# Two row gathers of a large expert slot, held back until the next small slot's first and last gelu

## The reference, cut to what matters

```python
xn = _layernorm(x)
g, v, d = xn @ Wg + bg, xn @ Wv + bv, xn @ Wd + bd
scan = linear_scan(sigmoid(g) * tanh(v), 0.001 + 0.998 * sigmoid(d))
scores = sigmoid(xn @ Wg_.T + bg_ + bias);  top 2 of 8 -> weights[T, E]
h  = gelu(einsum('td,ehd->teh', xn, W1) + b1)
eo = einsum('teh,edh->ted', h, W2) + b2
out = x + scan + gelu(xn @ Ws1.T + bs1) @ Ws2.T + bs2 + einsum('ted,te->td', eo, weights)
```

## Time and profile before

| what | value |
|---|---|
| time, 3 runs | median 681.78 us (680.64 to 683.04) |
| the profiled execution | 678.43 us, of it 676.6 us span |
| mean granted TensorE clock in it | 0.994 |
| busy share of the span | PE 95%, DVE 76%, ACT 64%, POOL 42% |

### The profile page before, as it was taken

The page is one execution under the profiler, slowest core; times in us unless marked ns, Lnnn a source line. Parts: engine busy times, 40 slices in busy tenths (PEclk is TensorE's granted clock), DMA queues, the critical chain, the costliest instruction groups (busy, mean ns, idle before and its releaser), DMA issues.

```text
span 676.6 us, 19821 instructions
## 1 busy us (share of the span) xinstructions
PE 642.1 (95%) x6246; PEld 505.7 (75%) x6247; DVE 513.3 (76%) x1328; ACT 435.6 (64%) x774; POOL 281.4 (42%) x263
## 2 busy tenths in 40 slices
PE   4899999999999999799999999999999999999993
PEld 3465757575656666588888888888888888888893
DVE  4899899999999989878666666666667667666772
ACT  6987786969696965455555545565566565656562
POOL 2133333324241515634454535344454636354432
PEclk9999999999999999999999999999999999999997
DMA  7525344342525141423333345355655666575622
GB/s 244 203 52 168 95 126 100 119 128 90 154 86 164 63 122 36 129 54 52 69 55 63 55 117 169 63 126 135 173 168 147 175 159 191 143 180 148 193 33 29
DMA packets 63264, 80.77 MB, mean 119 GB/s; under 512 B 19492, under 2 KB 55268, under 8 KB 60376
## 3 DMA queue, kind: packets, MB, share of 16 engines
q1 hardware_dynamic: 48072, 62.08, 28.8%
q0 software_dynamic: 15120, 17.77, 15.6%
HBM read 38.66 MB, written 18.10 MB: 84 GB/s over the span
## 4 chain that ended last, share of the span: by engine, by line
PE 79%; DVE 9%; issue 5%; ACT 3%; DMA 3%; DVEq 1%; POOL 0%; POOLq 0%; SPq 0%; ACTq 0%
PE bank L1320 30%; PE bank L1312 29%; PE bank L1300 7%; PE bank L1348 4%; PE bank L1371 3%; PE bank L1390 2%; DVE arena L941 2%; DVE arena L940 2%; DVE W L844 1%; ACT arena L641 1%; PE bank L1291 1%; DMA arena<-in_gates 1%; DVE arena L883 1%; PE bank L1256 1%; DMA out<-arena,slot_adds 1%
## 5 line engine op out<-in xcount | busy, mean ns | idle before, releaser
L1320 PE MATMUL bank<-W,arena 128*128 (+1 forms) x2112 | 277.1, 273 | 5.4 <-DVE arena L941 4.9
L1312 PE MATMUL bank<-rows,W 128*128 128x256 f16 (+1 forms) x1728 | 272.7, 296 | 4.7 <-issue 3.0
L641 ACT ACTIVATE arena<-bank,par 128x256 f32<-128x256 f32 (+2 forms) x344 | 164.5, 516 | 111.3 <-PE bank L1312 74.4
L1320 PEld LDWEIGHTS bank<-W,arena 128*128 128x128 f16 x2112 | 200.9, 98 | 42.1 <-issue 6.9
L1312 PEld LDWEIGHTS bank<-rows,W 128*128 (+1 forms) x1728 | 164.8, 98 | 58.9 <-issue 7.9
L555 POOL DMA_INDIRECT out<-arena,slot_adds x71 | 115.3, 1624 | 186.7 <-ACT arena L766 130.6
L940 DVE TENSOR_SCALAR arena<-arena,par 128x256 f16<-128x256 f32 (+1 forms) x284 | 102.3, 360 | 57.6 <-ACT arena L641 46.4
L941 DVE SCALAR_TENSOR_TENSOR arena<-arena,par 128x256 f16<-128x256 f32 (+1 forms) x284 | 133.9, 472 | 10.0
L499 POOL DMA_INDIRECT lists<-entry,place x64 | 70.6, 1103 | 125.1 <-ACT arena L623 66.5
L1300 PE MATMUL bank<-rows,W 128*128 128x512 f16 x288 | 63.8, 379 | 0.0
L647 ACT ACTIVATE rows<-bank 128x1024 f16<-128x1024 f16 (+2 forms) x43 | 36.1, 840 | 37.5 <-PE bank L1390 24.9
(11 more groups left out here) (189 smaller groups left out, 574.7 us busy)
## 6 DMA issues: line engine op xcount, KB each, us to landing
stage<-in_w SPq DMA_DIRECT2D x32, 512.0 KB
stage<-W SPq DMA_DIRECT2D x14, 1024.0 KB
arena<-W SPq DMA_DIRECT2D x8, 1024.0 KB
arena<-in_x SPq DMA_DIRECT2D x8, 512.0 KB
xhl_rows<-W SPq DMA_DIRECT2D x8, 512.0 KB, 3.7
out<-arena SPq DMA_DIRECT2D x8, 512.0 KB
b2row<-in_b SPq DMA_DIRECT2D x22, 128.0 KB
arena<-in_b SPq DMA_DIRECT2D x21, 128.0 KB
```

The source lines that it names most:

```text
L641: ins = A(h32[k][:, c], ps_e[k][:, c], ACT.Gelu, bias=p[:, 4 + e * i + jj:5 + e * i + jj], scale=p[:, 0:1])
L1312: ins = T.matmul(bank_, weights(w, wp * HALF + c * H + j * P, P), rhs[:, 2 * xp + c, :], start=n == 0, stop=n == 3 * KD - 1)
L1320: ins = T.matmul(banks[t // 2][:, (t % 2) * D:(t % 2 + 1) * D], h[:, hp, t * P:(t + 1) * P], weights(w, (2 + wp) * HALF + j * D, D), start ...
```

## The change

Inside `gather`, ahead of each of the two indirect DMAs of a large slot, a wait on `ev_act` is added, for large slots from 19 on. `small` is the slot after the one whose buffer is taken over (slot 16 for the gather of slot 19). The first DMA waits for the first gelu unit of `small`, the second for its last. Nothing else is changed: no DMA is added or taken away, and the order on GpSimd stays.

```diff
@@ -539,6 +539,10 @@
                     pool.wait_ge(r_ok, 2 * SEQS)
                 pool.wait_ge(rows_list_in[s.c], s.n // DEEP * 16 + 16)
                 for t in range(s.tiles):
+                    if s.rows == ROWS and s.n - DEEP >= FIRST + 1:
+
+                        small = order(s.n - DEEP + 1)
+                        pool.wait_ge(ev_act, RING + EV_A + small.unit + (1 if t == 0 else small.units))
                     pool.indirect_dma_start(
                         xg[s.c][0:s.parts, t, :], None, xhl_dram,
```

## The result

The changed kernel takes 674.54 us (673.96 to 674.79, five runs) against 683.04 us (680.64 to 683.86, five runs) for the kernel before: a ratio of 0.9879, with a 95% interval of 0.9859 to 0.9899. The prediction had 681.4 (679.8 to 683.4). The profiled execution of the changed kernel took 674.79 us, like its median; that of before, 678.43, was 4.6 us better than its own. So the two profiles show 3.6 of the 8.5 us, and the rest lies in executions that have no trace.

The account below looks back on a forecast made before the run. PE, busy for 95% of the span, was taken as the bound. Waits cost 0 and two freed splits save 0.21 + 0.21 us: 681.78 - 0.42 = 681.4 us, range 679.8 to 683.4.

Parts of the forecast that it names:

- The waits cost nothing: Gathers and scatter-adds delayed on GpSimd in LOW and MID turns would not make PE wait: cost 0.
- The held L940: In MID turns a GpSimd DMA lengthens DVE's split L940; freeing it would save 0.21 + 0.21 = 0.42 us in two turns.
- The reading of 475.97: PE's 0.40 us wait before 475.97 in the MID turn was put on the held L940 delaying L941; 0.21 us to gain.
- Nothing that the profile shows: Weight loads in the small slots' first layers wait 0.8 us with "issue" as cause, which nothing in the profile explains.
- the ceiling on the gain: All PE waits at L1371, the small slots' second layer, gone: 2.0 us, which gives the range's lower end, 679.8.
- Rival D: Faster: L1371's 2.0 us and the 0.8 us of "issue" waits go, as they fall beside gathers' traffic; 679.0, chance 0.10.
- That offset: The profiled execution of the kernel before took 678.43 us, 3.35 under the median of 681.78.
- A: Slower: moved DMAs hold slot 19's second split beyond PE's cover, up to 0.33 us in six MID turns; 683.8, chance 0.08.
- B: Slower: every L940 inside a moved gather is held to its end, twelve, 2.9 us less 0.4; 684.3, chance 0.02.
- C: No effect: PE's waits in MID turns come back at another place; 681.8, chance 0.20.

Follow-up runs that it names:

- e14: The kernel before with the second gather of each large slot from 19 on cut from 128 rows to 32: 680.98 us beside 681.37, ratio 0.9995.
- e0: The kernel before, unchanged, run again for a second profile: 673.86 us beside 674.04, ratio 0.9998.

## Why the prediction was wrong

**The waits cost nothing: right.** The second gather of slot 19 and scatter-add 15 came within 0.2 us of the forecast. The first gather of slot 19 went 1.0 us later (454.25 for 453.27). The second gather of the MID turn and scatter-add 17 behind it came 1.9 us earlier on the clock, because ACT's last gelu did, with the loss before it gone. Scatter-add 18 hit its forecast (483.39 for 483.3) by luck: it came 9.2 us after scatter-add 17, whose landing it waits for, not 7.2 as in before, and that made up for the 1.9 us. PE nowhere waits for a landing, and scatter-adds 15 and 19 weren't late.

**The held L940: the step that failed.** It was set at 0.42 us in two turns. L940 of the last unit is back at 0.35 in slot 18 (the 472.70 row above). But L1371's waits fell by 1.6 us (2.8 to 1.2), not by 0.4. The reading of 475.97 was wrong: I gave PE's 0.40 us to the last L940, 0.56 long, and did not ask why the gelu before it was late. The chain went back through weigh (472.91, itself after 2.08 us of idle time) to a result that DVE began 1.49 us after PE's end of the matmuls that it needs. On a quiet chip the same L940 took 0.65 us and PE didn't wait. So the hold of L940 is real, and what it was priced at belongs to the late result before it.

**"Nothing that the profile shows", and the ceiling on the gain: wrong too.** The 0.8 us of the earlier trace rows and PE's stop at 454.39 were set aside as no one's. In four LOW turns of that trace PE goes on after such a stop 1.4 to 1.5 us after the start of the second gather. And L1371's 2.0 us were called nearly all that PE loses to the order of work at the small slots, which gave the lower end of the range. PE's lost time fell by 3.6 us in the profiles alone. Rival D, with a chance of 0.10, comes nearest: it had both terms go, 2.8 us in all. Its reason, traffic of the gathers, was not what ran: a quarter of the rows changed nothing (e14). Even so 8.5 us between the medians are more than the two profiles account for. The profiled execution of before lies 4.6 us below its median and 2.2 below the fastest of the five runs. That offset was in the prediction as 3.35 us, and I took the sum over it unchanged; a cost that varies from run to run can be larger in the runs without a trace. How the remaining 4.9 us divide stays open.

**A, B and C.** A's mechanism appears once in the rows shown (the L944 at 473.49 held by 0.18) without reaching PE. B, the page's rule of the Trainium skill ("SBUF — State Buffer") that the loser blocks for the whole instruction, doesn't fit that row: L944 takes 0.35 and ended at 474.02, so it got through at 473.67, 0.26 us before the gather's end at 473.93. C had PE's waits come back at another place, and in part they did: those at the second layer of large slots rose from 0.9 to 1.9 us while L1371's fell. C's number, no effect, was also measured for parts of the change on quiet chips, but for another reason: there was no late result there to begin with.

## What to carry to other kernels

When an engine starts late, look at when the instruction that it needs ended. The releaser that the view names may be a later one, and if the engine starts right behind a counter that moved late, the delay is ahead of it. If several engines are late at the same moment, look at which other instruction ran then. In these traces the costly place for a GpSimd indirect DMA was right at the end of a matmul group that another engine waits for, or beside PE's smallest groups. And before trusting a gain of a per cent, run the kernel before in more than one place. This change is worth 1% in some batches, and its parts were worth nothing in others. Moving one DVE instruction on top of it was worth 0.46% there.

## What the runs showed of the hardware

The same program took 674.0 us in some batches and 679.7 to 683.0 in others, with the granted clock at 0.99 in both. In the latter, PE stops inside its groups, its signals to DVE and ACT come up to 1.7 us late, and some of SP's register instructions take over 60 ns longer than their median, near GpSimd's indirect DMAs; in none of the ten profiles from quiet chips do the long register instructions appear. The signature is in the counters, too: the ten traces from disturbed chips keep 8149 to 8451 movements of them, the ten from quiet chips 9843 to 10014. A longer L940 beside a GpSimd DMA instruction is another thing and is found on both kinds (675 ns at most in before, 718 in e0). With 19 weight copies thinned, 5.9 us of the time are gone, though the result is still late in the MID turns; with a quarter of the second gather's rows, none of it. Which part of the chip carries the hold, and what makes a chip disturbed, was not shown.
